# Causal attention scores on 64-row parts of TensorE's array, with the sums of the preceding block at the end of a block

## The reference

```python
qkv = x @ w_qkv
q, k, v = jnp.split(qkv, 3, axis=-1)
q, k, v = (to_heads(q), to_heads(k), to_heads(v))      # (B, 16, T, 8)
q = q * cos + _rotate_half(q) * sin
k = k * cos + _rotate_half(k) * sin
att = jnp.einsum('bhtd,bhsd->bhts', q, k) * scale
att = jnp.where(causal, att, jnp.finfo(att.dtype).min)
att = jax.nn.softmax(att, axis=-1)
y = jnp.einsum('bhts,bhsd->bhtd', att, v)
```

## Time and profile before

| | before |
|---|---|
| median of 3 runs | 713.02 us (710.68 to 713.17) |
| the profiled execution | 713.36 us, of which the span from first to last instruction is 711.6 us |
| mean granted TensorE clock | 0.957 of full speed |
| busy share | PE 89%, PEld 65%, DVE 69%, ACT 50%, POOL 23% |

### The profile page before, as it was taken

How to read it: one execution, slowest core, us unless ns; L and a number is a source line. 1 busy time by engine, 2 the same in 40 slices (tenths; PEclk the granted TensorE clock), 3 DMA queues, 4 the chain that set the end, 5 groups by cost and what they waited for, 6 DMA issues and landing times.

```text
span 711.6 us, 11849 instructions
## 1 busy us (share of the span) xinstructions
PE 630.4 (89%) x4028; PEld 459.5 (65%) x4028; DVE 491.2 (69%) x1528; ACT 357.0 (50%) x727; POOL 162.9 (23%) x290
## 2 busy tenths in 40 slices
PE   1877677969999987799998989999999998999998
PEld 1756566858887975465555555555656554788887
DVE  3568883755877759977765657787887831777765
ACT  3744335312323464166668767666566676332221
POOL 4573354250003540001524240112211000100000
PEclk9999979969999995789999999999999999999999
DMA  7000000032232200000000000000000000333342
GB/s 271 1 1 1 1 0 1 1 120 82 100 118 68 87 29 0 1 1 1 1 1 1 0 1 1 2 0 1 2 1 1 1 2 16 105 110 105 117 136 75
DMA packets 18667, 27.88 MB, mean 39 GB/s; under 512 B 2984, under 2 KB 7208, under 8 KB 18608
## 3 DMA queue, kind: packets, MB, share of 16 engines
q1 hardware_dynamic: 17888, 25.85, 11.1%
q10 hardware_dynamic: 720, 1.28, 0.5%
HBM read 25.79 MB, written 1.33 MB: 38 GB/s over the span
## 4 chain that ended last, share of the span: by engine, by line
PE 68%; DVE 12%; ACT 3%; issue 3%; POOL 3%; DMA 1%; SPq 0%; DVEq 0%; POOLq 0%
PE bank L1583 12%; PE bank L1611 10%; PE bank L1541 10%; PE bank L1481 9%; PE bank L1271 6%; PE bank L1273 6%; PE bank L1272 6%; PE bank L1593 2%; DVE hn L882 2%; DVE bank L1154 1%; DVE work L1157 1%; PE bank L1551 1%; PE bank L1510 1%; PE bank L1522 1%; PE bank L1279 1%
## 5 line engine op out<-in xcount | busy, mean ns | idle before, releaser
L791 ACT ACTIVATE arena<-bank 128x512 f32<-128x512 f32 (+3 forms) x384 | 166.9, 493 | 88.2 <-PE bank L1593 64.8
L1154 DVE CUSTOM_DVE_ANT_0 bank<-bank,mask_qk 128x512 f32<-128x512 f32 (+3 forms) x256 | 121.1, 512 | 47.6 <-PE bank L1611 46.6
L1611 PE MATMUL bank<-kza,qta 128*128 128x512 f32 (+3 forms) x320 | 126.5, 409 | 4.9 <-DVE work L1154 1.3
L1583 PE MATMUL bank<-qtb,kza 128*128 128x512 f32 (+3 forms) x320 | 120.1, 387 | 2.0 <-DVE work L1154 1.0
L718 ACT ACTIVATE work<-bank 128x512 f32<-128x512 f32 x80 | 47.7, 598 | 121.0 <-PE bank L1273 115.6
L1157 DVE TENSOR_REDUCE work<-bank 128x1 f32<-128x512 f32 x128 | 81.6, 684 | 24.4 <-PE bank L1611 23.8
L1583 PEld LDWEIGHTS bank<-qtb,kza 128*128 128x128 f32 x320 | 60.4, 191 | 57.5 <-ACT arena L791 51.6
L1481 PE MATMUL bank<-dw,work 128*128 128x128 f32 x640 | 87.1, 281 | 6.1 <-DVE work L1084 6.1
L1481 PEld LDWEIGHTS bank<-dw,work 128*128 128x128 f32 x640 | 83.5, 196 | 10.4 <-issue 6.3
L1080 DVE TENSOR_TENSOR work<-work,bank 128x512 f32<-128x512 f32 x80 | 54.9, 686 | 50.7 <-PE bank L1273 45.9
L1541 PE MATMUL bank<-arena 128*9 128x512 f32 (+3 forms) x768 | 79.9, 488 | 0.4 <-ACT arena L791 0.4
(11 more groups left out here) (193 smaller groups left out, 1149.0 us busy)
## 6 DMA issues: line engine op xcount, KB each, us to landing
kt<-cw_rows SPq DMA_DIRECT2D x160, 128.0 KB, 2.9
x<-x_in SPq DMA_DIRECT2D x4, 256.0 KB, 8.8
y_out<-x SPq DMA_DIRECT2D x4, 256.0 KB, 3.1
arena<-gw_in SPq DMA_DIRECT2D x1, 640.0 KB, 8.8
arena<-uw_in SPq DMA_DIRECT2D x1, 640.0 KB, 8.4
dw<-dw_in SPq DMA_DIRECT2D x1, 640.0 KB, 9.4
work<-q_in SPq DMA_DIRECT2D x2, 256.0 KB, 6.6
arena<-wa_in ACTq DMA_DIRECT2D x1, 393.0 KB, 7.0
```

What stands on the lines that cost most here:

```text
L791: act.activation(pb[:, blk % 2, h, 0:w], s_bank(n)[:, 0:w], ACT.Exp, scale=SCALE).then_inc(p_ready, 1)
L1154: ins = dve.tensor_tensor_reduce(out=src, in0=src, in1=mask_qk[:, CW - w:], scale=1.0, scalar=-3e38, op0=ALU.add, op1=ALU.max, accum_out=dst)
L1583: ins = pe.matmul(s_bank(n)[:, 0:w], kz(s, h, j // CT)[:, j % CT * P:(j % CT + 1) * P], qtb[:, s % 2, (c + 1) * CW - w:(c + 1) * CW], star ...
L1611: pe.matmul(a_bank(n)[:, 0:w], qta[:, slot(b, g), i * P:(i + 1) * P], kz(s, h, half)[:, 0:w], start=True, stop=True).then_inc(a_full, 1)
```

## The change

The rows of a group are split in two pairs of 64: heads 0 and 1 on rows 0 to 63, heads 2 and 3 on rows 64 to 127. `pair(h)` is that slice, and `score`, `score_max` and `mask` now contract over those 64 rows alone. Key tiles of two heads in different pairs share one tile, so `kza` alone holds all, and `uh`, `ul`, their two memsets and the semaphore `kz_clear` are out. The heads are taken in other orders (`S_HEADS`, `A_HEADS`), so that neighbouring matmuls mostly stand in different pairs of rows. A mask is now two matmuls of 64 columns with 64 rows each in place of one of 128 columns. `BLOCK_ORDER` puts the sums of the preceding block behind all scores, masks and maxima; they stood ahead of the fourth score.

```diff
-C_ID, C_MA, C_MB, C_BM, C_HS, C_IO, C_COS, C_SIN, C_END = 0, 128, 256, 384, 512, 528, 544, 608, 672
+C_ID, C_MA, C_MB, C_BM, C_HS, C_IO, C_COS, C_SIN, C_END = 0, 128, 256, 512, 640, 656, 672, 736, 800
-BLOCK_ORDER = (("score", 0), ("max", 0), ("score", 1), ("mask", 0), ("mask", 1), ("max", 1), ("score", 2),
-               ("mask", 2), ("max", 2), ("sums", None), ("score", 3), ("mask", 3), ("max", 3))
+S_HEADS, A_HEADS = (0, 2, 1, 3), (2, 0, 3, 1)
+BLOCK_ORDER = (("score", 0), ("max", 0), ("max", 1), ("score", 1), ("mask", 0), ("mask", 1), ("score", 2),
+               ("max", 2), ("mask", 2), ("max", 3), ("score", 3), ("mask", 3), ("sums", None))
...
-        kza = [sb(f"kza{i}", [P, GH, CW], F32R) for i in range(3)]
+        kza = sb("kza", [P, 4, 2, CW], F32R)
...
-            if s % 2 == 0 and half:
-                return (uh, ul)[h // 2][:, h % 2 * CW:(h % 2 + 1) * CW]
-            return kza[0 if s % 2 == 0 else 1 + half][:, h, :]
+            return kza[:, 2 * (s % 2) + half, h % 2, :]
+
+        def pair(h):
+
+            return slice(h // 2 * 2 * SL, (h // 2 + 1) * 2 * SL)
...
-                dve.wait_ge(qkv_full, TB)
-                dve.memset(uh[:, 0:2 * CW].bitcast(F32), 0.0)
-                dve.memset(ul[:, 0:2 * CW].bitcast(F32), 0.0).then_inc(kz_clear, 1)
...
-                    ins = pe.matmul(s_bank(n)[:, 0:w], kz(s, h, j // CT)[:, j % CT * P:(j % CT + 1) * P],
-                                    qtb[:, s % 2, (c + 1) * CW - w:(c + 1) * CW], start=True, stop=True)
+                    ins = pe.matmul(s_bank(n)[:, 0:w], kz(s, h, j // CT)[pair(h), j % CT * P:(j % CT + 1) * P],
+                                    qtb[pair(h), s % 2, (c + 1) * CW - w:(c + 1) * CW], start=True, stop=True)
...
-                        pe.matmul(s_bank(n)[:, 0:P], identb[:, :], mask_kq[:, :], start=False, stop=True,
-                                  skip_group_check=True).then_inc(b_full, 1)
+                        for a in range(2):
+                            ins = pe.matmul(s_bank(n)[:, a * 2 * SL:(a + 1) * 2 * SL], mask_kq[r, a, :], identb[r, r],
+                                            start=False, stop=True, skip_group_check=True)
+                        ins.then_inc(b_full, 1)
...
-                    pe.matmul(a_bank(n)[:, 0:w], qta[:, slot(b, g), i * P:(i + 1) * P],
-                              kz(s, h, half)[:, 0:w], start=True, stop=True).then_inc(a_full, 1)
+                    pe.matmul(a_bank(n)[:, 0:w], qta[pair(h), slot(b, g), i * P:(i + 1) * P],
+                              kz(s, h, half)[pair(h), 0:w], start=True, stop=True).then_inc(a_full, 1)
```

More of the change, by code:

```diff
@@ L209, in macaron @@
         identb = sb("identb", [P, P], BF16)
-        mask_kq = sb("mask_kq", [P, P], BF16)
+        mask_kq = sb("mask_kq", [P, 2, P], BF16)
         mask_qk = sb("mask_qk", [P, CW], BF16)
@@ L333, in macaron @@
             sem("qkv_full"), sem("qkv_ready"), sem("v_ready"))
-        stg_clear, kz_clear, kz_ready = sem("stg_clear"), sem("kz_clear"), [sem(f"kz_ready{s}") for s in range(STEPS)]
+        stg_clear, kz_ready = sem("stg_clear"), [sem(f"kz_ready{s}") for s in range(STEPS)]
         kt_full, kt_ready = sem("kt_full"), sem("kt_ready")
@@ L566, in _ @@
                     pool.memset(stm[:, :, :, :, :].bitcast(F32), 0.0)
-                    for z in kza:
-                        pool.memset(z[:, :, :].bitcast(F32), 0.0)
+                    pool.memset(kza[:, :, :, :].bitcast(F32), 0.0)
             for i in range(TB):
@@ L766, in alone @@
                     act.wait_ge(kt_ready, 2 * (TB * b + CT * (half + 1)))
-                    if s == 0 and half:
-                        act.wait_ge(kz_clear, 1)
                     if s >= 2:
@@ L785, in causal @@
                             w = min(CW, CW * (c + 1) - j * P)
-                            for h in range(GH):
-                                n = blk * GH + h
+                            for i, h in enumerate(S_HEADS):
+                                n = blk * GH + i
                                 act.wait_ge(b_full, n + 1)
-                                if h == 0 and blk >= 2:
+                                if i == 0 and blk >= 2:
                                     act.wait_ge(pv_done, blk - 1)
@@ L1146, in maxima @@
                 w = min(CW, (i + 1) * P - half * CW)
-                for h in range(GH):
-                    n = (s * NBLK + k) * GH + h
+                for order, h in enumerate(A_HEADS):
+                    n = (s * NBLK + k) * GH + order
                     dve.wait_ge(a_full, n + 1)
@@ L1158, in maxima @@
                     ins.then_inc(a_free, 1)
-                    if h == 1:
+                    if order == 1:
                         drains(s - 1, k)
@@ L1570, in causal, with score @@
             def causal():
-                def score(s, k, h):
+                def score(s, k, order):
                     c, j = B_BLOCKS[k]
                     b, g = divmod(s, G)
-                    n = (s * NBLK + k) * GH + h
+                    h = S_HEADS[order]
+                    n = (s * NBLK + k) * GH + order
                     w = min(CW, CW * (c + 1) - j * P)
-                    if h == 0:
+                    if order == 0:
                         pe.wait_ge(qtb_ready, 2 * s + c + 1)
@@ L1620, in causal @@
                         now, ahead = s >= 0, s + 1 < STEPS
-                        for kind, h in BLOCK_ORDER:
+                        for kind, order in BLOCK_ORDER:
                             if kind == "score" and now:
-                                score(s, k, h)
+                                score(s, k, order)
                             if kind == "mask" and now:
-                                mask(s, k, h)
+                                mask(s, k, order)
                             if kind == "max" and ahead:
-                                score_max(s + 1, k, h)
+                                score_max(s + 1, k, order)
                             if kind == "sums" and now and s * NBLK + k >= 1:
@@ L1672, in constants @@
     c[:, C_MA:C_MA + P] = np.where(r[None, :] > r[:, None], -1e30, 0.0)
-    c[:, C_MB:C_MB + P] = np.where(r[:, None] > r[None, :], -1e30, 0.0)
+    for a in range(2):
+        c[:, C_MB + a * P:C_MB + (a + 1) * P] = np.where(r[None, :] > (r[:, None] % (2 * SL) + a * 2 * SL), -1e30, 0.0)
     c[:, C_BM:C_BM + P] = r[:, None] // HD == r[None, :] // HD
```

16 lines of the change are left out of this document (9 added, 7 removed).

## The result

The changed kernel takes **748.79 us** (median of 4 runs, 742.59 to 750.79) against 713.1 (4 runs) before: a ratio of 1.049, with a 95% interval of 1.046 to 1.053. I had forecast 702.5 and faster. The prediction was wrong in sign, by 46 us. The profiled execution of the changed kernel took 750.79 us, its span is 749.0 us and its mean granted clock 0.877; before it was 0.957.

The account below looks back on a forecast made before the run. TensorE was taken to bound the causal stage, VectorE not far behind. Blocks -12.3, tasks +4.0, memsets -1.6 and slow clock -1.0 summed to -10.9 us; the forecast was 713.0 - 10.5 = 702.5 us, range 690 to 716.

Parts of the forecast that it names:

- What bounds the kernel, and the loop that takes over: Causal stage: TensorE bounds it; then a loop through banks and VectorE's maximum sets unmasked blocks, 3.03 to 2.75 us.
- Overlap of parts: Neighbouring matmuls on different rows run together: a 512-wide pair costs 0.23 us in place of 0.47.
- Narrow blocks: Blocks where a matmul already costs 0.11 us: no gain taken; their shrinking was named a sign of being wrong.
- My rival with weights side by side: Weights load side by side and mode changes are free; narrow blocks shrink some 0.3 us each; 688 us, 14%.
- Masks: Two 64-column mask matmuls cost what one of 128 columns did, so 0; otherwise 17 us, about half hidden.
- Memsets and the start: Dropped VectorE memsets on the chain give -1.6 us; pairs at half clock before and at step 0's start, -1.0.
- Sums at the end: Moved sums cost 0, the loop crossing them once either way; tasks behind sums at 0.08 add +4.0 us.
- The change of shape: Full-height task between sums and next block's first score: 0 to 0.20 us each, taken as 0.08, about 50 blocks.
- A first score behind a task of over 0.4: Named sign of being wrong: the first score after a task takes over 0.4 us.
- steps 1 and 2 keep their length: Named sign of being wrong; half the gain was taken in steps 1 and 2, which hold the second batch's projections.
- The clock: A clock falling back because fewer rows are fed was counted only inside the no-overlap rival, 723 us, 15%.
- a rival of 15%: No overlap in time: 3.03 us blocks stay, tasks cost 4, masks 8; also covers a falling clock; 723 us, 15%.

Follow-up runs that it names:

- experiment 9: Changed kernel, sums at the end only in blocks without a small task: 707.43 us; only in blocks with one: 752.15 us.
- experiment 3: Changed kernel with the block order of before, so 64-row parts but sums ahead of the fourth score: 706.96 us, ratio 0.988.
- experiment 1: Changed kernel with heads in plain order 0, 1, 2, 3, so neighbouring matmuls mostly share their 64 rows: 835.82 us.
- experiment 2: Kernel before, full height, with only the block order changed to sums at the end: 727.9 us against 712.0, ratio 1.020.
- Experiment 5: Kernel before, only the scores of step 7 contract over 64 rows in place of 128: 738.31 us against 713.31.
- experiment 7: Kernel before, sums at the end only in 43 blocks without a small task: 711.47 us, ratio 0.999; only in 53 with one: 730.88, ratio 1.024.
- experiment 8: Changed kernel, old order, one extra pair of second score and score_max per block, three score copies in step 7: 702.12 us, same as without those three.
- the last experiment: Changed kernel, sums at the end only in the 53 blocks with a small task, old order elsewhere: 752.15 us (735.45 to 759.72).

## Why the prediction was wrong, step by step

- **What bounds the kernel, and the loop that takes over:** right. 2.72 us a block where I had 2.75, with VectorE's maximum ahead of the fourth `score_max`, as named. (The lower bound of that loop adds up to 2.63, not the 2.65 I wrote; and of the -10.9 of the sum I took 10.5 off the median. Nothing hangs on either.)
- **Overlap of parts:** right for 512 columns; starts lie 0.00 apart. The term was too small rather than too large. In step 6, at full clock, the parts save 3.1 us (experiment 9) where I had 2.04. By an estimate at 5 us for each 0.01 of clock: experiment 3 ran at 0.92 and the kernel before at 0.957, which is 18 us, so at equal clock the parts would be worth some 5 + 18 = 23 us and not 14.9 (overlap, memsets, slow clock at the start).
- **Narrow blocks: wrong, on the good side.** I took no gain where a matmul already costs 0.11 and named shrinking narrow blocks as a sign of being wrong. They shrank. The first scores of blocks 10 and 11 and of the next step, on the changed kernel's chain, with the four masks behind the last:

```profile
592.11 0.31 PE bank L1581
...
594.31 0.25 PE bank L1581
...
596.06 0.42 PE bank L1581 x2
596.49 0.13 PE bank L1593 x4
```

Block 10 takes 2.20 us for 2.43, block 11 1.75 for 1.91. It is the overlap that does it: in experiment 1, where neighbours share their rows, the same blocks at full clock take 2.44 and 1.98. My rival with weights side by side (14%) had this sign and the loads do start together; whether loads or matmuls save the time, no run tells.
- **Masks:** right. The four matmuls of 64 columns in a row take 0.13 (above), as two of 128 columns did.
- **Memsets and the start:** no run shows the 2.6 us that I took for them. The first score of the stage starts at 301.18 us before and at 300.01 in the changed kernel, but between 299.26 and 300.93 in the full-height kernels of experiments 2, 5 and 7, which keep the memsets.
- **Sums at the end: wrong, and the first of two steps that failed.** I wrote that "the loop of three crosses the sums once in either order: 0" and took the tasks at +0.08 each. The first half holds for blocks without a task (experiment 7: 0.999). With a task the loop also crosses the task: 53 blocks cost 18.3 us at full height, 0.35 each, where I had a change of shape in mind and not a longer loop. In the old order the fourth score and `score_max` stand between sums and task, and their exponential and maximum, which the loop needs next, run beside the task; with the sums at the end the task stands between the sums and the next block's first score and `score_max`, and holds both back.
- **The change of shape:** at full height it costs nothing more. The task behind the sums takes 0.59 and the score behind it 0.23, before they were 0.39 and (ahead of it) 0.43: 0.82 both times, shown below. With the parts the score behind the task takes 0.43 again (546.81 above), so 0.20 more, the upper bound of my range and not 0.08. For some 50 tasks that is 10 us by an estimate, where I took 4.0. A first score behind a task of over 0.4 was a sign of being wrong that I had named; so was that steps 1 and 2 keep their length, and step 1, at full clock, took 42.90 us for 42.00.

The chain of experiment 2, the task behind the sums and the first score:

```profile
564.72 0.98 PE bank L1541 x8
565.69 0.59 PE bank L1522 x4
566.29 0.28 PE bank L1524
566.57 0.23 PE bank L1583
```

and of the kernel before, the same task in its old place:

```profile
552.28 0.98 PE bank L1541 x8
553.26 0.43 PE bank L1583
...
553.91 0.39 PE bank L1522 x4
```

The Trainium skill's rule (TensorEngine Tiling (Array Packing), Key Properties) that a change of mode drains the array agrees with the 0.20, and I should have followed it.

- **The clock: wrong, and the larger step.** I had it inside a rival of 15%, and set against it that "the clock stays at 1.00 in step 7 where TensorE waits in each block". Step 7 fed 128 rows; that row says nothing about 64. Experiment 5 changes this alone and the stage falls to 0.50. In the changed kernel two things come together: half the rows, and longer waits, above all in the blocks with a task. The order alone left the clock at 0.96 (experiment 2), the parts alone took it to 0.92 (experiment 3), both together to 0.88. At 4.7 to 5.4 us for each 0.01, the 0.078 between experiment 2 (0.959) and the changed kernel (0.881) are 37 to 42 us by an estimate. With the 23 us from experiment 3 and the 16 of the order this makes 713 - 23 + 16 + 37 to 42 = 743 to 748, and up to 53 x 0.20 = 11 us more where a task's change of shape stands on the chain; measured are 748.8.

What stays open: how the terms of the last sum divide exactly, since clock and waits feed each other; which waits make up the rest of the loss in experiment 2; whether the clock answers to the number of rows or to the split of the array; and why experiment 8 gained nothing. That a task ahead of the fourth score, with the sums still at the end, would cost less was not tried.

## What to carry to other kernels

Row parts cut what TensorE needs, but the same cut can lower the clock that it is granted: count a gain from fewer rows only after a run has shown the clock with those rows, and if it falls, unneeded matmuls in the gaps may pay (30 us here, though that kernel was still slower than the one before, 718.9 for 712.0). When a stage is bound by a loop between engines, list everything that stands in the loop in each kind of block, the rare small tasks too: moving sums past them cost nothing in 43 blocks and 18 us in 53. And a clock read in one stage is evidence only for the same rows and columns.

## What the hardware showed that I had not expected

- Two matmuls on different 64 rows start within 0.01 us of each other, with both weight loads (0.18 us each) beside each other.
- At the same instructions, order and columns, 64 rows in place of 128 in one step took the granted clock from 1.00 to 0.50 behind 36.50 us without a gap in TensorE's work. The kernel went from 713.31 to between 737.79 and 742.43 us in three runs of four; the fourth took 718.77.
- A kernel on one core has no single time at such a point: the six runs of the last experiment spread over 24 us, and followed the clock (735.45 at 0.901, 759.72 at 0.849).
- Blocks of 256 and 128 columns also got shorter when neighbours stood on different rows (2.43 to 2.20 and 1.91 to 1.75 us), and not when they shared them (2.44 and 1.98).
- From a full-height task back to 64-row matmuls costs 0.20 us (0.43 in place of 0.23 for the first score).
